# Table sets, first decays and the weight gathers of a one-core decoder layer: an order rewritten around the state scan

## The chip, the core and the metric

One core of a Trainium2 chip runs the whole layer as one program. The metric is device microseconds of one execution; lower is better. Engines are named as in the profile: PE (matrix multiply), DVE (vector), ACT (scalar functions), POOL (GpSimd), SP (a queue that only issues transfers). ACT and POOL issue transfers too.

## What is computed

The layer is `x = layernorm(x + f(x))` three times, on 4 x 256 tokens of width 256, for three functions `f`:

```
# 1: a state space block (512 channels, 16 states) and a mixture of experts behind it
x, z = split(rmsnorm(h) @ in_proj.T);  xc = silu(conv4(x) + conv_b)
dt, B, C = split(xc @ x_proj.T) ;  dt = softplus(rmsnorm(dt) @ dt_proj.T + dt_b)
h_t = h_{t-1} * exp(dt_t * A) + (dt_t * x_t) * B_t ;  y_t = sum_n h_t * C_t      # the scan
r = (y + xc * D) * silu(z) @ out_proj.T + h
logits = rmsnorm(r) @ router.T ; top 2 of 8 experts ; sum of w2(silu(w1 t) * w3 t)
# 2: cross attention over 64 keys, 16 heads
# 3: a feed forward block in fp8: columns of w_gate, w_up and w_down are reordered by index
#    tables, every row is scaled by its largest size and rounded to fp8
g = q(x[:, up]) @ q(w_gate[:, up]).T ; u likewise with w_up ; y = q((silu(g) * u)[:, down]) @ q(w_down[:, down]).T
```

Softplus is computed as `max(v, 0) + log(1 + exp(-|v|))`, so each part of `dt` passes through `Abs`, `Exp` and `Ln` on ACT, with a correction of the rounding on DVE between `Exp` and `Ln`.

## The kernel before

Each engine has its own program, written out by hand; semaphores order them against each other. The sequence has these stages.

**Projections (to 74 us).** The tokens are taken in two halves of 512, the 512 channels in four chunks of 128. ACT's order mixes `Silu` (convolution, `take_gates` 0 to 3), `Exp` (`dt_exponential`) and `Ln` (`dt_logarithm`). Whenever ACT needs a function that is not in the table set it holds, the compiler puts a table load ahead of it. On DVE `rounding_rest`, `softplus` and `scan_inputs` follow ACT; PE transposes the products `dt * x` (`transpose_inputs`) and `take_inputs` copies them from PSUM to SBUF as `dtxT`: tiles 0 to 3 on DVE, 4 to 7 on ACT.

**The scan (74 to 224 us).** There are 64 units: 2 halves x 16 states x 2 pairs of channel chunks. For each unit ACT makes the decays `exp(dt * A)` (`decay_of`, two instructions of 510 columns) and scales rows of `dtxT` by `B` (`input_rows`, three of 512 columns and one diagonal of 128 for each two units); PE turns these rows (`inputs_of`); DVE runs `tensor_tensor_scan` over 1024 columns (`scan_of`), with the decays from SBUF and the inputs from PSUM; POOL multiplies the states by `C` (line 470, 1024 columns, both operands in SBUF); PE adds the products up (`sum_states`). `decay_of(u)` waits for scan `u-2`, scan `u` for product `u-3`. The last product is done by DVE (`last_state_times_c`, line 1318).

**Behind the scan (224 to 258 us).** PE projects the gated result, DVE adds it to `x` and finds the two best experts of each token. From there DVE alone counts, ranks and places the tokens in a chain of small instructions, each waiting for the one before (lines 1341 to 1382; among them `place + behind`, line 1362, `picked * place`, line 1363, and 16 comparisons, line 1374). PE gathers from these marks the row indices, and POOL uses them in `gather_rows` (line 487), with which the experts begin.

**Weight gathers.** `w_up` and `w_gate` (6 chunks of 128 rows each) are gathered through `down_reorder_index` by POOL with one indirect transfer for each chunk. In this kernel POOL issues all 12 before the scan, into spare memory (`got`), because their final place `w_raw` is taken by `dt` until the last decay is made. Behind the scan `mask_up` multiplies them by a mask of columns into `w_raw` (lines 454), then `w_down` is masked (line 480), then come two small powers for the norm of the result (line 484). SP starts the load of the second expert's weights, which lie over part of `got`, when all three masks are done.

Of the kernel before, what the change touches and what calls it, by code (L numbers as in the profile page):

```python
# [43 lines left out]
KVT = BATCH * KV  # L44
FPAD = FCH * P
FP8_MAX = 448.0
SCALES = 2 * FCH + KD


# [17 lines left out]
def build(nc, inp, out):  # L67
    with ExitStack() as ctx:
# [116 lines left out]
        up_mask, down_mask = sb("up_mask", [P, D]), view(118, [FF], BF16)  # L185
        count_row = view(159, [FF + D], rows=1)
        w_raw = [view(72.5, [FCH, D]), view(78.5, [FCH, D]), view(112.5, [KD, FF])]
        got = [view(16.5, [FCH, D]), (view(146.5, [4, D]), view(22.5, [2, D]))]
        w_size = [view(66.5, [FCH * D]), view(66.5, [FCH * D]), view(66.5, [KD * FF])]
        w_fp8 = [view(34.5, [FCH, D], BF16), view(37.5, [FCH, D], BF16), view(181, [KD, FPAD], BF16)]  # L190
        w_fp8T = [view(73.5, [KD, FPAD], BF16), view(76.5, [KD, FPAD], BF16), view(84.5, [FCH, D], BF16)]
# [86 lines left out]
        def _(sp):  # L278
# [47 lines left out]
            for m in range(C_BUFS, 2 * NS):  # L326
                sp.wait_ge(s["hc_done"], 2 * (m - C_BUFS) + 2)
                load_c_row(m)
            sp.wait_ge(s["masked"], 3)
            load_weights(1)  # L330
            for half in range(2):
                tiles = slice(half * HALF_TILES, (half + 1) * HALF_TILES)
# [37 lines left out]
        def _(pool):  # L370
# [78 lines left out]
                    pool.indirect_dma_start(dst[:, c - chunks[0], :], None, inp[name], bass.IndirectOffsetOnAxis(gather_at[:, c:c + 1].bitcast(U32), 0))\  # L449
                        .then_inc(s[f"gathered_w{m}"], 16)  # L450

            def mask_up(dst, rows, chunks, gathered):
                pool.wait_ge(s[gathered], FCH * 16)
                pool.tensor_tensor(dst, rows, up_mask[:, :].unsqueeze(1).to_broadcast([P, chunks, D]), ALU.mult).then_inc(s["masked"], 1)

            pool.wait_ge(s["ld_idx"], 16)
            pool.wait_ge(s["xproj_psum"], 2 * CI)
            pool.wait_ge(s["dt_psum"], 2 * CI)
            gather_weights(1, "w_up", range(4), got[1][0])
            pool.wait_ge(s["z_psum"], TILES)  # L460
            gather_weights(1, "w_up", range(4, FCH), got[1][1])
            gather_weights(0, "w_gate", range(FCH), got[0])
            in_chunks = lambda v: v.rearrange("p (c t) -> p c t", c=2)
            for unit in range(UNITS - 1):
                m = unit // 2
# [6 lines left out]

            pool.wait_ge(s["da_ready"], UNITS)
            pool.wait_ge(s["scan_done"], UNITS + 1)
            mask_up(w_raw[1][:, 0:4, :], got[1][0], 4, "gathered_w1")
            mask_up(w_raw[1][:, 4:FCH, :], got[1][1], FCH - 4, "gathered_w1")
            mask_up(w_raw[0], got[0], FCH, "gathered_w0")
            pool.wait_ge(s["spread_done"], 2)
            pool.wait_ge(s["ld_late"], 32)
            pool.tensor_tensor(w_raw[2], w_raw[2], down_mask.unsqueeze(1).to_broadcast([P, KD, FF]), ALU.mult).then_inc(s["masked"], 1)  # L480
            for half in range(2):
                tiles = slice(half * HALF_TILES, (half + 1) * HALF_TILES)
                pool.wait_ge(s["ms_ready"], 7 + half)
                pool.tensor_tensor(rs[:, tiles], ms[:, tiles], neg_half[:, tiles], ALU.pow).then_inc(s["rstd"], 1)

            def gather_rows(index):
                pool.indirect_dma_start(row_in, None, hn_rows[:, :], bass.IndirectOffsetOnAxis(index, 0)).then_inc(s["ld_rows"], 16)  # L487
# [100 lines left out]
        def _(act):  # L588
# [67 lines left out]
            def dt_exponential(c, half):  # L656
                act.wait_ge(s["dt_act"], CI * half + c + 1)
                nc.scalar.activation(u[half][:, c, :], u[half][:, c, :], ACT.Exp, scale=-1.0).then_inc(s["dt_exp"], 1)
# [21 lines left out]
                for n in range(HALF_TILES, TILES):  # L680
                    nc.scalar.activation(zsT[:, n, :], zsT[:, n, :], ACT.Silu).then_inc(s["z_out"], 1)

            def take_inputs(i):
                act.wait_ge(s["dtxT_psum"], 2 * CI)
                tile = HALF_TILES + i
                nc.scalar.activation(dtxT[:, tile, :], ps[:, tile, :], ACT.Identity).then_inc(s["dtxT_done"], 1)


# [56 lines left out]
            take_dt(2, 0)  # L745
            convolved(2, 1)
            convolved(3, 1)
            dt_exponential(0, 0)
            squares_of_small(1)
            take_small(1)  # L750
# [6 lines left out]
            take_gates(1)  # L757
            take_gates(2)
            take_gates(3)
            dt_logarithm(0, 0)  # L760
            take_dt(0, 1)
            dt_logarithm(1, 0)
# [14 lines left out]
            dt_logarithm(0, 1)  # L777
            dt_logarithm(1, 1)
            take_gates(6)
            dt_logarithm(2, 1)  # L780
            dt_logarithm(3, 1)
            take_gates(7)
            act.wait_ge(s["routing"], RATES_READY)
            act.wait_ge(s["consts"], 5)
            act.wait_ge(s["softplus"], 2)
            decay_of(0)
            act.wait_ge(s["b_scaled"], 2)
            input_rows(0, range(HALF_TILES))
            act.wait_ge(s["softplus"], 4)
            decay_of(1)  # L790
            act.wait_ge(s["ld_idx"], 32)
            act.wait_ge(s["routing_psum"], 3)
            input_rows(1, range(HALF_TILES))
            for i in range(HALF_TILES):
                take_inputs(i)
            act.wait_ge(s["softplus"], 2 * CI)
            act.wait_ge(s["b_scaled"], 4)
            for unit in range(2, UNITS):
                decay_of(unit)
                if unit // 2 + 1 < 2 * NS:  # L800
                    input_rows(unit // 2 + 1, range(2 * (unit % 2), 2 * (unit % 2) + 2))

# [268 lines left out]
        def _(dve):  # L1071
# [126 lines left out]
                dve.wait_ge(s["conv_out"], n + 1)  # L1198
                nc.vector.tensor_tensor(dtx[half][:, c, :], dt[:, c, halves[half]], xc[:, c, halves[half]], ALU.mult).then_inc(s["dtx_done"], 1)

            def take_inputs(i):
                dve.wait_ge(s["dtxT_psum"], CI)
                nc.vector.tensor_copy(dtxT[:, i, :], ps[:, i, :]).then_inc(s["dtxT_done"], 1)

            def take_routing():
                dve.wait_ge(s["routing_psum"], 3)
                link(nc.vector.tensor_tensor(x_rms[:, :], ms[:, 0:TILES], rs[:, 0:TILES], ALU.mult))
# [47 lines left out]
            take_routing()  # L1255
            rounding_rest(2, 1)
            softplus(0, 1)
            take_inputs(0)
            take_inputs(1)
            take_inputs(2)  # L1260
            take_inputs(3)
            softplus(1, 1)
            scan_inputs(0, 1)
            scan_inputs(1, 1)
# [6 lines left out]
            def quantise(m, parts):  # L1271

                chunks, width = (FCH, FCH, KD)[m], (D, D, FF)[m]
                w, size = w_raw[m], w_size[m].rearrange("p (a b) -> p a b", b=width)
                largest, inverse, scale = (v[:, m, 0:chunks] for v in (w_max, w_inv, w_scale))
                if 1 in parts:
                    dve.wait_ge(s["masked"], (3, 2, 4)[m])
                    link(nc.vector.tensor_reduce(largest, w, axis=AX.X, op=ALU.max, apply_absolute_value=True))
                    link(nc.vector.tensor_scalar(scale, largest, 1.0 / FP8_MAX, None, ALU.mult))
                    link(nc.vector.reciprocal(inverse, scale))  # L1280
                if 2 in parts:
                    for c in range(chunks):
                        ins = nc.vector.tensor_scalar(w[:, c, :], w[:, c, :], inverse[:, c:c + 1], None, ALU.mult)
                    ins.then_inc(s["w_scaled"], 1)
                if 4 in parts:
                    dve.wait_ge(s["w_sized"], (2, 3, 1)[m])
                    link(nc.vector.scalar_tensor_tensor(w, size, LEAST_ADDED, w, ALU.max, ALU.add))
                if 5 in parts:
                    ins = nc.vector.scalar_tensor_tensor(w_fp8[m][:, :, 0:width], size, LEAST_ADDED, w, ALU.max, ALU.subtract)
# [1157 lines left out]
```

## Time and profile before

| | us |
|---|---|
| three runs: median (lowest to highest) | 630.99 (630.53 to 631.51) |
| the profiled execution, its own time | 630.9 |
| its span from first to last instruction | 628.9 |
| projections, up to the first scan | 74.3 |
| 64 scans and the last product, up to | 226.7 |
| first rows of the experts requested | 255.1 |

All times in the rows are microseconds from the start of the span. 2.0 us of the profiled execution lie outside the span. A timeline row gives the start, the time from the first instruction's start to the last one's end, engine, line, operation, output and inputs, the count, and in brackets the idle time before it and what ended that.

### The profile page before, as it was taken

The page shows a single profiled execution, that of the slowest core. Times are in us where ns is not written, and L with a number is a line of the kernel's source. Part 1 is how long each engine was busy: PE and PEld are TensorE (multiplying, and loading weights), DVE is VectorE, ACT ScalarE, POOL GpSimd, SP SyncE. Part 2 cuts the span into 40 slices and gives each one's busy share as a digit, 9 for nine tenths or more (in the row PEclk, how much of TensorE's full clock was granted, in tenths as well). Part 3 has the DMA queues.
Part 4 walks back from the last instruction along what each step waited for, and adds up shares of the span by engine and source line. Part 5 has one row for each costly group of instructions (what it writes and reads, how often), then busy time and mean ns, then how long its engine had stood idle before and what let it go on. Part 6 is the DMA issues. An engine that isn't in the chain of part 4 may idle for free.

```text
span 628.9 us, 10914 instructions
## 1 busy us (share of the span) xinstructions
PE 583.5 (93%) x3632; PEld 440.8 (70%) x3632; DVE 464.5 (74%) x786; ACT 385.7 (61%) x879; POOL 301.5 (48%) x242
## 2 busy tenths in 40 slices
PE   6999689998999999999999999999999999998774
PEld 3553589887998887597779779778845555665442
DVE  6989999999999976544553543553555789998875
ACT  5689899999999956522232231321745764687633
POOL 7022699999999991134232334344112332225201
PEclk9999899999999999999999999999999999999998
DMA  8001651111221108334441441441510000000001
GB/s 288 1 2 43 203 194 52 53 66 51 52 67 51 34 17 327 125 124 172 172 158 49 172 170 35 169 177 30 160 45 1 1 2 0 1 1 1 2 0 67
DMA packets 18432, 52.41 MB, mean 83 GB/s; under 512 B 3872, under 2 KB 9647, under 8 KB 16720
## 3 DMA queue, kind: packets, MB, share of 16 engines
q1 hardware_dynamic: 15344, 42.36, 19.3%
q0 software_dynamic: 2752, 7.34, 3.9%
q10 hardware_dynamic: 288, 2.10, 0.9%
q8 instruction: 26, 0.43, 0.3%
q14 instruction: 22, 0.18, 0.1%
HBM read 47.13 MB, written 4.67 MB: 82 GB/s over the span
## 4 chain that ended last, share of the span: by engine, by line
PE 69%; ACT 13%; DVE 10%; issue 5%; DMA 2%; POOL 1%; SPq 0%; POOLq 0%; DVEq 0%; ACTq 0%
PE ps L2165 12%; PE ps L2230 8%; ACT arena L699 7%; PE ps L2173 6%; PE ps L2219 4%; PE ps L2251 4%; ACT arena L714 3%; PE ps L1948 3%; PE ps L1933 3%; PE ps L2105 3%; PE ps L1982 2%; PE ps L1782 2%; PE ps L1791 2%; PE ps L2031 2%; PE ps L1935 2%
## 5 line engine op out<-in xcount | busy, mean ns | idle before, releaser
L470 POOL TENSOR_TENSOR arena<-arena 128x1024 f32<-128x1024 f32 x63 | 147.3, 2389 | 3.3 <-DVE arena L1301 3.0
L1301 DVE TENSOR_TENSOR_SCAN arena<-arena,ps 128x1024 f32<-128x1024 f32 x64 | 143.4, 2279 | 4.0 <-ACT arena L699 0.9
L699 ACT ACTIVATE arena<-arena,a_neg 128x510 f32<-128x510 f32 x128 | 84.5, 708 | 1.9 <-DVE arena L1301 1.7
L2165 PEld LDWEIGHTS ps<-arena 128*128 128x128 f32 x660 | 75.5, 192 | 3.5 <-issue 3.1
L2165 PE MATMUL ps<-arena 128*128 128x128 f32 x660 | 77.1, 276 | 0.0
L1933 PE MATMUL ps<-ident,arena 128*128 128x128 f32 x384 | 64.7, 278 | 9.9 <-ACT arena L710 8.5
L1948 PE MATMUL ps<-ident,arena 128*128 128x128 f32 x512 | 67.3, 273 | 2.5 <-DVE arena L1310 1.8
L910 ACT ACTIVATE arena<-ps 128x256 f32<-128x256 f32 x45 | 17.3, 384 | 82.1 <-PE ps L2165 82.1
L714 ACT ACTIVATE arena<-arena,b_tok 128x512 f32<-128x512 f32 x96 | 64.8, 708 | 0.0
L1948 PEld LDWEIGHTS ps<-ident,arena 128*128 128x128 f32 x512 | 57.8, 141 | 4.1 <-DVE arena L1310 1.3
L2230 PE MATMUL ps<-arena 128*128 128x512 f32 x128 | 58.2, 595 | 0.0
L1933 PEld LDWEIGHTS ps<-ident,arena 128*128 128x128 f32 x384 | 45.8, 143 | 14.6 <-ACT arena L710 12.8
L1935 PE MATMUL ps<-arena 128*128 128x128 f32 x256 | 50.0, 277 | 0.0
L549 POOL TENSOR_TENSOR q_rs<-q_ms,neg_half 128x16 f32<-128x16 f32 x8 | 23.6, 2948 | 50.8 <-DVE q_ms L1552 50.8
L936 ACT ACTIVATE arena<-ps 128x128 f32<-128x128 f32 x128 | 33.5, 279 | 22.1 <-PE ps L2230 22.1
L2173 PE MATMUL ps<-arena 128*128 128x256 f32 x180 | 41.3, 379 | 0.0
L2230 PEld LDWEIGHTS ps<-arena 128*128 128x128 f32 x128 | 23.5, 190 | 24.1 <-issue 21.3
L520 POOL DMA_INDIRECT moe_out<-arena,result_now x23 | 24.1, 1047 | 32.3 <-DVE arena L1488 20.5
L1935 PEld LDWEIGHTS ps<-arena 128*128 128x128 f32 x256 | 39.2, 193 | 0.0
L1480 DVE TENSOR_TENSOR arena<-arena,ps 128x256 f32<-128x256 f32 x30 | 12.6, 422 | 34.5 <-ACT arena L910 33.1
L2173 PEld LDWEIGHTS ps<-arena 128*128 128x128 f32 x180 | 33.0, 190 | 3.9
L487 POOL DMA_INDIRECT arena<-hn_rows,row_now x23 | 25.4, 1106 | 18.2 <-POOL row_now L505 18.2
(316 smaller groups left out, 1135.8 us busy)
## 6 DMA issues: line engine op xcount, KB each, us to landing
arena<-in_w_moe SPq DMA_DIRECT2D x8, 2176.0 KB, 9.0
arena<-c_dram SPq DMA_DIRECT2D x32, 256.0 KB, 3.2
arena<-in_w_o ACTq DMA_DIRECT2D x1, 2048.0 KB, 13.1
arena<-in_w_qT SPq DMA_DIRECT2D x1, 2048.0 KB, 10.0
arena<-in_w_q SPq DMA_DIRECT2D x1, 2048.0 KB, 8.0
arena<-moe_out SPq DMA_DIRECT2D x8, 256.0 KB, 4.5
x<-in_x SPq DMA_DIRECT2D x2, 512.0 KB, 4.6
arena<-in_w_in SPq DMA_DIRECT2D x2, 512.0 KB, 5.8
```

What stands on the lines that cost most here:

```text
L470: pool.tensor_tensor(in_chunks(hC[unit % 3]), in_chunks(h[unit % 3]), c_bc[:, m % C_BUFS, :].unsqueeze(1).to_broadcast([P, 2, HALF]), ALU. ...
L487: pool.indirect_dma_start(row_in, None, hn_rows[:, :], bass.IndirectOffsetOnAxis(index, 0)).then_inc(s["ld_rows"], 16)
L699: ins = nc.scalar.activation(dA_b[:, unit % 2, 2 * k:2 * k + 2, 1:], dt_b[:, c, 2 * half:2 * half + 2, 1:], ACT.Exp, scale=a_neg[:, c, n:n ...
L714: nc.scalar.activation(sdtx[m % 2][:, i, :], dtxT[:, HALF_TILES * half + i, :], ACT.Identity, scale=b_tok[:, HALF_TILES * half + i, n:n + ...
L936: ins = nc.scalar.activation(q_junk[:, g % 2, hd * DH:(hd + 1) * DH], ps[:, g % 2, hd * DH:(hd + 1) * DH], ACT.Square, scale=float(DH) ** ...
L1301: nc.vector.tensor_tensor_scan(h[unit % 3], dA[:, k, :], ps[:, 2 * k:2 * k + 2, :].rearrange("p a b -> p (a b)"), 0.0, ALU.mult, ALU.add). ...
L1933: ins = nc.tensor.transpose(dst, sdtx[m % 2][:, i, c * P:(c + 1) * P], ident[:, :])
L1935: ins = nc.tensor.matmul(dst, dtxT[:, HALF_TILES * half + i, c * P:(c + 1) * P], b_diag[m % 2], start=True, stop=True)
L1948: return nc.tensor.matmul(ps[:, bank, c * P:(c + 1) * P], part, ident[:, :], start=first, stop=last, is_transpose=ADD_TRANSPOSED, skip_gro ...
L2165: ins = nc.tensor.matmul(ps[:, bank, c * P:(c + 1) * P], w13[:, k, chunk * P:(chunk + 1) * P], xT[:, k, :], start=(k == 0), stop=(k == KD ...
L2173: ins = nc.tensor.matmul(ps[:, 6, 0:D], hid[:, c, :], w2[:, c, :], start=(c == 0), stop=(c == FCH - 1))
L2230: ins = nc.tensor.matmul(ps[:, g % 2, :], tokens(t, k), w_q[:, k, g * HALF:(g + 1) * HALF], start=(k == 0), stop=(k == KD - 1))
```

## The change

- ACT is told twice to load a set that holds both `Exp` and `Ln`: ahead of the first `dt_exponential` and, behind the `Silu` of the gates, ahead of the first `dt_logarithm`.
- On ACT `decay_of(0)` and `decay_of(1)` come ahead of the last two logarithms; the copies `take_inputs` of tiles 0 to 3 leave DVE and come on ACT ahead of the first `input_rows`; those of tiles 4 to 7 come behind `decay_of(2)`.
- Before the scan POOL gathers only four chunks of `w_up`. The other two and all six of `w_gate` are gathered behind the scan, straight into `w_raw`, where they are masked in place. POOL's order behind the scan becomes: mask four chunks, gather 2 + 4, power of the first half, gather 2, mask two chunks, power of the second half, mask `w_down`, mask the six chunks of `w_gate`.
- SP starts the load of the second expert when 63 products are done.

```
@@ POOL, before the scan
-            gather_weights(1, "w_up", range(4), got[1][0])
-            pool.wait_ge(s["z_psum"], TILES)
-            gather_weights(1, "w_up", range(4, FCH), got[1][1])
-            gather_weights(0, "w_gate", range(FCH), got[0])
+            gather_weights(1, "w_up", range(4), got_up)
@@ POOL, behind the scan
             pool.wait_ge(s["scan_done"], UNITS + 1)
-            mask_up(w_raw[1][:, 0:4, :], got[1][0], 4, "gathered_w1")
-            mask_up(w_raw[1][:, 4:FCH, :], got[1][1], FCH - 4, "gathered_w1")
-            mask_up(w_raw[0], got[0], FCH, "gathered_w0")
+            mask_up(w_raw[1][:, 0:4, :], got_up, "gathered_w1", 4)
+            gather_weights(1, "w_up", range(4, FCH), w_raw[1][:, 4:FCH, :])
+            gather_weights(0, "w_gate", range(4), w_raw[0][:, 0:4, :])
+            rstd_of_result(0)
+            gather_weights(0, "w_gate", range(4, FCH), w_raw[0][:, 4:FCH, :])
+            mask_up(w_raw[1][:, 4:FCH, :], w_raw[1][:, 4:FCH, :], "gathered_w1", FCH)
+            rstd_of_result(1)
             pool.wait_ge(s["spread_done"], 2)
             pool.wait_ge(s["ld_late"], 32)
             pool.tensor_tensor(w_raw[2], w_raw[2], down_mask..., ALU.mult).then_inc(s["masked"], 1)
-            for half in range(2):
-                ...
+            mask_up(w_raw[0], w_raw[0], "gathered_w0", FCH)
@@ SP
-            sp.wait_ge(s["masked"], 3)
+            sp.wait_ge(s["hc_done"], UNITS - 1)
             load_weights(1)
@@ ACT
+            nc.scalar.preload_act_table_set(EXP_AND_LOG)
             dt_exponential(0, 0)
...
+            nc.scalar.preload_act_table_set(EXP_AND_LOG)
             dt_logarithm(0, 0)
...
             take_gates(6)
-            dt_logarithm(2, 1)
-            dt_logarithm(3, 1)
-            take_gates(7)
...
             decay_of(0)
+            act.wait_ge(s["softplus"], 4)
+            decay_of(1)
+            dt_logarithm(2, 1)
+            dt_logarithm(3, 1)
+            take_gates(7)
+            for i in range(HALF_TILES):
+                take_inputs(i)
             act.wait_ge(s["b_scaled"], 2)
             input_rows(0, range(HALF_TILES))
-            act.wait_ge(s["softplus"], 4)
-            decay_of(1)
...
             input_rows(1, range(HALF_TILES))
-            for i in range(HALF_TILES):
-                take_inputs(i)
...
                 decay_of(unit)
+                if unit == 2:
+                    for i in range(HALF_TILES, TILES):
+                        take_inputs(i)
@@ DVE: the four take_inputs between softplus(0, 1) and softplus(1, 1) are gone;
   quantise waits for "masked" 4, 2, 3 (w_gate, w_up, w_down) in place of 3, 2, 4
```

## Rows read from the trace of the kernel before

**Rows 1.** The page's chain that ended last, by engine.
```profile
PE 69%; ACT 13%; DVE 10%; issue 5%; DMA 2%; POOL 1%; SPq 0%; POOLq 0%; DVEq 0%; ACTq 0%
```

**Rows 2.** The chain of waits from 222 to 262 us: start, length, what.
```profile
223.64 1.97 DVE arena L1318
...
251.81 2.35 PE ps L2051 x16
...
255.10 3.09 DMA arena<-hn_rows,row_of
```

**Rows 3.** ACT's timeline ahead of the scan and in its first units.
```profile
55.45 1.28 ACT L658 ACT_TABLE_LOAD   x1
...
61.38 1.28 ACT L662 ACT_TABLE_LOAD   x1
...
66.07 1.28 ACT L699 ACT_TABLE_LOAD   x1
...
70.44 0.39 ACT L710 ACTIVATE arena<-ident,b_tok 128x128 f32<-128x128 f32 x1
...
76.27 2.06 ACT L686 ACTIVATE arena<-ps 128x512 f32<-128x512 f32 x4 [2.09 <-PE ps L1841]
...
80.65 1.33 ACT L699 ACTIVATE arena<-arena,a_neg 128x510 f32<-128x510 f32 x2
```

**Rows 4.** DVE's timeline up to the first scans.
```profile
66.68 2.47 DVE L1203 COPY arena<-ps 128x512 f32<-128x512 f32 x4
...
73.63 0.23 DVE L1167 TENSOR_TENSOR b_tok<-b_tok,rs 128x64 f32<-128x64 f32 x1
74.29 4.46 DVE L1301 TENSOR_TENSOR_SCAN arena<-arena,ps 128x1024 f32<-128x1024 f32 x2 [0.44 <-PE ps L1935]
79.65 33.06 DVE L1301 TENSOR_TENSOR_SCAN arena<-arena,ps 128x1024 f32<-128x1024 f32 x14 [0.89 <-ACT arena L699]
```

**Rows 5.** PE's timeline around the first scans.
```profile
70.41 1.72 PE L1841 MATMUL ps<-ident,arena 128*128 128x128 f32 x8 [4.28 <-DVE arena L1199]
...
82.94 0.55 PE L1933 MATMUL ps<-ident,arena 128*128 128x128 f32 x3 [1.87 <-ACT arena L710]
```

**Rows 6.** Windows of PE: length, busy, granted clock, DMA share, GB/s.
```profile
71.00:72.00 1.00, 1.00 (x7) 0.50 0.09 20
```

**Rows 7.** POOL's timeline: last gather, products of the scan, masks, powers.
```profile
73.99 0.94 POOL L449 DMA_INDIRECT arena<-in_w_gate,index_at  x1 [0.30 <-issue]
...
82.02 77.61 POOL L470 TENSOR_TENSOR arena<-arena 128x1024 f32<-128x1024 f32 x33 [0.65 <-DVE arena L1301]
...
226.81 6.99 POOL L454 TENSOR_TENSOR arena<-arena,up_mask 128x1024 f32<-128x1024 f32 x3 [1.22 <-issue]
233.76 2.86 POOL L480 TENSOR_TENSOR arena<-arena 128x1408 f32<-128x1408 f32 x1
239.63 1.04 POOL L484 TENSOR_TENSOR rs<-ms,neg_half 128x4 f32<-128x4 f32 x1 [3.01 <-DVE ms L1330]
246.37 1.01 POOL L484 TENSOR_TENSOR rs<-ms,neg_half 128x4 f32<-128x4 f32 x1 [5.70 <-DVE ms L1330]
```

**Rows 8.** DVE's timeline behind the scan: the last product and two placing steps.
```profile
223.64 3.04 DVE L1318 TENSOR_TENSOR arena<-arena 128x1024 f32<-128x1024 f32 x1
...
247.92 0.23 DVE L1362 TENSOR_TENSOR place<-place,behind 128x64 f32<-128x64 f32 x1
248.18 0.29 DVE L1363 TENSOR_TENSOR picked<-picked,place 128x128 f32<-128x128 f32 x1
```

**Rows 9.** Line 1561: duration in ns, least, median and most, of eight.
```profile
L1561 DVE TENSOR_TENSOR arena<-arena,total_e x8: 1224/1226/2066, 478.0 to 587.1; 128x1024 f32<-128x1024 f32 x8
```

**Rows 10.** DVE's timeline, 536 to 542 us, attention and feed forward.
```profile
539.17 2.07 DVE L1561 TENSOR_TENSOR arena<-arena,total_e 128x1024 f32<-128x1024 f32 x1
```

**Rows 11.** POOL's timeline, 476 to 560 us, the same place.
```profile
538.48 1.67 POOL L560 TENSOR_TENSOR arena<-arena 128x704 f32<-128x704 f32 x1 [6.95 <-ACT arena L963]
```

**Rows 12.** Line 449, the weight gathers: time from issue to landing.
```profile
DMA to landing us min/median/max: 2.7/3.0/10.2
```

More of the change, by code:

```diff
@@ L46 @@
 FP8_MAX = 448.0
+EXP_AND_LOG = "natural_log_exp_and_others"
 SCALES = 2 * FCH + KD
@@ L187, in build @@
         w_raw = [view(72.5, [FCH, D]), view(78.5, [FCH, D]), view(112.5, [KD, FF])]
-        got = [view(16.5, [FCH, D]), (view(146.5, [4, D]), view(22.5, [2, D]))]
+        got_up = view(146.5, [4, D])
         w_size = [view(66.5, [FCH * D]), view(66.5, [FCH * D]), view(66.5, [KD * FF])]
@@ L450, in gather_weights, with mask_up @@
                         .then_inc(s[f"gathered_w{m}"], 16)
-            def mask_up(dst, rows, chunks, gathered):
-                pool.wait_ge(s[gathered], FCH * 16)
-                pool.tensor_tensor(dst, rows, up_mask[:, :].unsqueeze(1).to_broadcast([P, chunks, D]), ALU.mult).then_inc(s["masked"], 1)
+            def mask_up(dst, rows, gathered, landed):
+                pool.wait_ge(s[gathered], landed * 16)
+                pool.tensor_tensor(dst, rows, up_mask[:, :].unsqueeze(1).to_broadcast([P, rows.shape[1], D]), ALU.mult).then_inc(s["masked"], 1)
             pool.wait_ge(s["ld_idx"], 16)
@@ L474, in _, with rstd_of_result @@
             pool.wait_ge(s["scan_done"], UNITS + 1)
-            mask_up(w_raw[1][:, 0:4, :], got[1][0], 4, "gathered_w1")
-            mask_up(w_raw[1][:, 4:FCH, :], got[1][1], FCH - 4, "gathered_w1")
-            mask_up(w_raw[0], got[0], FCH, "gathered_w0")
+            mask_up(w_raw[1][:, 0:4, :], got_up, "gathered_w1", 4)
+            gather_weights(1, "w_up", range(4, FCH), w_raw[1][:, 4:FCH, :])
+            gather_weights(0, "w_gate", range(4), w_raw[0][:, 0:4, :])
+            def rstd_of_result(half):
+                tiles = slice(half * HALF_TILES, (half + 1) * HALF_TILES)
+                pool.wait_ge(s["ms_ready"], 7 + half)
+                pool.tensor_tensor(rs[:, tiles], ms[:, tiles], neg_half[:, tiles], ALU.pow).then_inc(s["rstd"], 1)
+            rstd_of_result(0)
+            gather_weights(0, "w_gate", range(4, FCH), w_raw[0][:, 4:FCH, :])
+            mask_up(w_raw[1][:, 4:FCH, :], w_raw[1][:, 4:FCH, :], "gathered_w1", FCH)
+            rstd_of_result(1)
             pool.wait_ge(s["spread_done"], 2)
@@ L480, in _ @@
             pool.tensor_tensor(w_raw[2], w_raw[2], down_mask.unsqueeze(1).to_broadcast([P, KD, FF]), ALU.mult).then_inc(s["masked"], 1)
-            for half in range(2):
-                tiles = slice(half * HALF_TILES, (half + 1) * HALF_TILES)
-                pool.wait_ge(s["ms_ready"], 7 + half)
-                pool.tensor_tensor(rs[:, tiles], ms[:, tiles], neg_half[:, tiles], ALU.pow).then_inc(s["rstd"], 1)
+            mask_up(w_raw[0], w_raw[0], "gathered_w0", FCH)
             def gather_rows(index):
@@ L681, in late_gates, with take_inputs @@
                     nc.scalar.activation(zsT[:, n, :], zsT[:, n, :], ACT.Silu).then_inc(s["z_out"], 1)
-            def take_inputs(i):
-                act.wait_ge(s["dtxT_psum"], 2 * CI)
-                tile = HALF_TILES + i
+            def take_inputs(tile):
+                act.wait_ge(s["dtxT_psum"], CI if tile < HALF_TILES else 2 * CI)
                 nc.scalar.activation(dtxT[:, tile, :], ps[:, tile, :], ACT.Identity).then_inc(s["dtxT_done"], 1)
@@ L1199, in scan_inputs @@
                 nc.vector.tensor_tensor(dtx[half][:, c, :], dt[:, c, halves[half]], xc[:, c, halves[half]], ALU.mult).then_inc(s["dtx_done"], 1)
-            def take_inputs(i):
-                dve.wait_ge(s["dtxT_psum"], CI)
-                nc.vector.tensor_copy(dtxT[:, i, :], ps[:, i, :]).then_inc(s["dtxT_done"], 1)
             def take_routing():
@@ L1257, in _ @@
             softplus(0, 1)
[L1258 to L1261, printed above, removed]
             softplus(1, 1)
@@ L1276, in quantise @@
                 if 1 in parts:
-                    dve.wait_ge(s["masked"], (3, 2, 4)[m])
+                    dve.wait_ge(s["masked"], (4, 2, 3)[m])
                     link(nc.vector.tensor_reduce(largest, w, axis=AX.X, op=ALU.max, apply_absolute_value=True))
```

## The prediction

> **What bounds the kernel now.** I read the page's chain first: PE carries most of it [rows 1], so any delay ahead of the experts goes through PE to the end. The change touches two stretches, so next came the timelines of ACT, DVE and PE up to the first scans, and of POOL and DVE behind the scan, with the chain of waits there.
>
> In the first stretch ACT works without a break and pays 1.28 us for each table load, three of them after 55 us [rows 3]. DVE has its own work done at 73.86 [rows 4]. The first scan, at 74.29, waits 0.44 us for PE [rows 4]; PE had stood still for 4.28 us and then ran at a granted clock of 0.50, which is 1.2 of 2.4 GHz [rows 5, 6]. The third scan waits another 0.89 us for its decays [rows 4], because ACT's copies of tiles 4 to 7, from 76.27, are ahead of them [rows 3].
>
> In the scan itself POOL has no room: 33 products in 77.61 us are 2.35 each [rows 7], against 2.36 for DVE's early scans (33.06 for 14) [rows 4]. What comes earlier at its start comes earlier at its end.
>
> Behind it the chain runs over the last product, PE's projections, and then DVE's placing steps, PE's 16 small matmuls at 251.81 and the request for rows at 255.10 [rows 2]. POOL has done its masks by 236.62 (233.76 + 2.86) and then waits for DVE [rows 7]: its masks end long before DVE's first placing step.
>
> **The change, part 1: the start of the scan.** *ACT.* From the first of the three loads, 55.45, to the end of the first diagonal, 70.73, ACT needs 15.28 us [rows 3]. Three loads with their gaps of 0.02 go: -3.9. Two things are moved ahead: one more pair of decays, about 1.22 by the pitch of such pairs (1.33 from first start to last end, less 0.1 of overlap), and four copies, 2.06 [rows 3]. 55.45 + 15.28 - 3.9 + 1.22 + 2.06 = 70.1. Being earlier, ACT meets PE's results at two places (the rows of C and the seventh gate); I add 0.3: 70.4. The two early decays wait for nothing late, since the first half of `dt` is done by then; behind them the two logarithms meet DVE's second rounding steps, which finish at about the same time.
>
> *DVE.* Four copies go. They take 2.47 us, 2.4 of pitch [rows 4], so DVE is ready at 73.86 - 2.4 = 71.5. *PE.* The transposes that waited for DVE come 2.4 us earlier, and PE's break ahead of them shrinks from 4.28 to about 1.9. After a break of 1.87 us three transposes took 0.55 us, full speed [rows 5]. The inputs of the first unit then start at 70.4, with ACT's diagonal, and take some 1.15 us, to 71.6: the first scan starts at 71.7, 2.6 us earlier. If PE is at half clock still, add 1.15: 72.8.
>
> *The next scans.* Its first scan ends at 71.7 + 2.23 (half of 4.46 [rows 4]) = 73.95. Then ACT makes decays (1.22), four copies (2.06), two rows (1.22), decays (1.22): 79.7 for the decays of the fourth unit. Before, that pair began at 80.65 [rows 3] and was done at 81.87. The order behind it is as before, so the gain that stays is **2.15 us**; the wait of 0.89 has only moved from the third scan to the fourth. Bounds: 1.1 with PE at half clock, 2.4 if nothing but DVE's copies counted. POOL agrees: its fourth product starts at about 82.15 instead of 82.02 + 2.35 = 84.37. POOL's eight gathers ahead of the scan end at 74.93 [rows 7]; they had to go, as the first product is wanted at 73.95, a cost of 1.0 avoided, not a further gain.
>
> The Trainium skill, "ScalarE: Activation LUTs", section "What ACT_TABLE_LOAD costs", gives 2.66 us for a switch with a drain of 1.38. This trace shows 1.28 and the next instruction 0.02 behind it. By the page ACT would come 4.1 us earlier still, and the scan would start with DVE at 71.5 in place of 71.7.
>
> **Part 2: POOL behind the scan** (times of the kernel before; all of it moves 2.15 earlier together). The masks take 6.99 us for 3072 columns, 2.28 ns each [rows 7]. From 226.81: mask of four chunks 2.33, to 229.1. Six gathers, 0.94 plus 0.30 of issue [rows 7], 7.5 with their first, to 236.7. The first power waits until 239.63 as before: cover 2.9 us. Two gathers, to 243.2; mask of two chunks 1.17, to 244.4. The second power starts at 246.37 as before: cover 2.0, so the norm and the stored rows are not late. Up to here the moved work costs nothing; without the covers it would be paid in full.
>
> Then come the mask of `w_down`, 247.4 to 250.3, and that of six chunks of `w_gate`, 1536 x 2.28 = 3.5 us, to 253.8. Both read two operands from SBUF, and now run beside DVE's placing steps, which begin at 247. Three rows show what that does. Line 1318, two SBUF operands of 1024 columns, took 3.04 us while POOL's last product ran [rows 8]; line 1561, the same shape, takes 1.23, except 2.07 in the worst case [rows 9], and that one started at 539.17 inside a POOL product from 538.48 to 540.15 [rows 10, 11]: 540.15 + 1.23 is its end within 0.15. So DVE waited for the end of POOL's instruction each time.
>
> Line 1362 (two SBUF operands, 247.92 [rows 8]) would therefore wait from 247.9 to 250.3, and line 1363, 0.26 behind it, for the second mask: 250.5 + 3.5 = 254.0 instead of 248.18 [rows 8]. The chain behind it is unhindered again. Term: **+5.8 us**. It hardly matters who wins between the masks, since the chain can't be through before the second has ended. Bounds: 5.4 if `w_gate` runs at the rate of `w_down` (2.86 for 1408 columns, 2.03 ns: 3.1 us [rows 7]), 6.0 if DVE is caught a step earlier; 0 if small steps are let through, which no row shows. I take 5.8, as every row of this pair of engines is a full wait. Queued behind: PE waits with its 16 matmuls [rows 2], POOL's own request for rows waits for DVE anyway, and ACT's exponential for the router waits with them.
>
> The Trainium skill, "SBUF — State Buffer", section "Who interferes with whom", has this as a rule: a DVE instruction with two SBUF inputs and a GpSimd instruction that reads SBUF exclude each other for the whole instruction. It speaks against this change; by it the sum is the one I make, without it 5.8 less.
>
> PE's break ahead of line 2051 grows from nothing to 5 us. After 4.28 us it ran at half clock [rows 5, 6]; the 16 matmuls take 2.35 us [rows 2] beside comparisons that DVE makes at about that pace. I take +0.4, between 0 and 2.3 (all of them twice as long).
>
> **At nothing:** the earlier load of the second expert (only earlier, and what SP has queued behind it waits for the norm anyway); the mask of `w_down` as third, since it is first wanted inside the experts; the load of `w_o`, which waits for the first mask, still the first.
>
> **Sum.** The profiled execution took 630.9 us, 628.9 of them its span; the median is 630.99, so nothing is to be corrected. 630.9 - 2.15 + 5.8 + 0.4 = **634.9 us**. Its own range: 630.9 - 2.4 + 5.4 = 633.9 to 630.9 - 1.1 + 6.0 + 2.3 = 638.1.
>
> **Rivals.** *A, the other side: DVE passes POOL.* If small placing steps aren't held up by the masks, only part 1 is left: 630.9 - 2.15 = 628.75. For it: the rows of waits are of 1024 columns, these steps have 64 and 128. Against it: a wait for a port doesn't ask how long the waiting one is. It decides once the hold is under 2.15 us.
>
> *B, only one mask bites.* Gathers land in 2.7 to 10.2 us [rows 12]; the last two are issued by 243.2, beside the load of `w_o`. If they land at about 253, DVE is held for the first mask alone, 2.4 us, and goes through before the second: 630.9 - 2.15 + 2.4 = 631.15. Against it: the median is 3.0 [rows 12].
>
> *C, the scan does not start earlier*, because the compiler puts loads back or ACT's new order is late elsewhere, while the masks bite: 630.9 + 5.8 + 0.4 = 637.1. Against it: PE's and DVE's waits at 74 go by count.
>
> **Chances.** About 0.2%, 1.3 us, is what a measurement of this kernel tells from no change. The forecast has 0.69, A 0.16, B 0.11, C 0.04. Faster 0.16 (A); same 0.11 (B); slower 0.73 (forecast and C). The range runs from 631.0 to 637.2: it takes in B, the forecast and C, and leaves out A and the top of the bounds.
>
> **What would show it.** Right: no table load on ACT between 50 and 74; the first scan near 71.7, a wait of about 1.3 ahead of the fourth; the last product some 2 us earlier; then line 1362 at about 2.6 us, line 1363 at about 3.5, PE standing still 5 us ahead of line 2051, and the first request for rows 3 to 4 us later than 255.10. Wrong: lines 1362 and 1363 at their old 0.23 and 0.29, or the second mask behind the request for rows.

## The result and the profile after

The changed kernel is slower: 639.09 us (median of four runs, 637.55 to 640.18) against 631.25 (median of four, 630.53 to 635.53). The ratio is 1.0105, 95% interval 1.007 to 1.0139. Forecast were 634.9 and a range up to 637.2: the sign came as forecast, and so did the hold of VectorE behind the scan, but the gain in the scan did not stay, and the time lies above the range.

The profiled execution took 639.09 us, its span 637.1. In the rows of after most line numbers are one higher than in those of before, POOL's and ACT's by other small amounts.

ACT's timeline ahead of the scan, answering to [rows 3]:

```profile
49.58 1.28 ACT L765 ACT_TABLE_LOAD   x1
50.88 0.63 ACT L667 ACTIVATE arena<-arena 128x512 f32<-128x512 f32 x1
...
70.41 0.41 ACT L714 ACTIVATE arena<-ident,b_tok 128x128 f32<-128x128 f32 x1
...
79.01 1.33 ACT L703 ACTIVATE arena<-arena,a_neg 128x510 f32<-128x510 f32 x2
```

The load at 49.58 is the last one, and the three behind 55 us are gone. The first diagonal is done at 70.82 (forecast 70.4), the fourth unit's decays at 80.34 (forecast 79.7); 0.48 us of each was lost ahead of the first `Exp` table load.

DVE's timeline, answering to [rows 4, 8]:

```profile
72.24 6.64 DVE L1302 TENSOR_TENSOR_SCAN arena<-arena,ps 128x1024 f32<-128x1024 f32 x3 [0.43 <-PE ps L1936]
80.43 4.52 DVE L1302 TENSOR_TENSOR_SCAN arena<-arena,ps 128x1024 f32<-128x1024 f32 x2 [1.55 <-ACT arena L703]
86.30 68.70 DVE L1302 TENSOR_TENSOR_SCAN arena<-arena,ps 128x1024 f32<-128x1024 f32 x30 [1.35 <-PE ps L1936]
...
157.29 2.28 DVE L1302 TENSOR_TENSOR_SCAN arena<-arena,ps 128x1024 f32<-128x1024 f32 x1
160.82 63.85 DVE L1302 TENSOR_TENSOR_SCAN arena<-arena,ps 128x1024 f32<-128x1024 f32 x28 [1.25 <-PE ps L1936]
224.70 2.69 DVE L1319 TENSOR_TENSOR arena<-arena 128x1024 f32<-128x1024 f32 x1
...
248.64 2.43 DVE L1363 TENSOR_TENSOR place<-place,behind 128x64 f32<-128x64 f32 x1
251.10 3.41 DVE L1364 TENSOR_TENSOR picked<-picked,place 128x128 f32<-128x128 f32 x1
...
260.95 0.19 DVE L1383 SCALAR_TENSOR_TENSOR result_of<-ps,row_of 128x34 uint32<-128x34 f32 x1
```

Read the brackets from above. The first scan starts 2.05 us earlier than in [rows 4]. The fourth, at 80.43, waits 1.55 for its decays. Then come two waits that before does not have, both for PE: 1.35 ahead of the sixth scan and 1.25 in the middle. So the last product, which began at 223.64 [rows 8], begins at 224.70, later and not earlier. Below it the two placing steps are held 2.43 and 3.41 us, where they took 0.23 and 0.29.

POOL's timeline behind the scan, answering to [rows 7]; POOL's mask at 248.13 and the next at 250.95 end where the two DVE steps end:

```profile
240.35 1.04 POOL L480 TENSOR_TENSOR rs<-ms,neg_half 128x4 f32<-128x4 f32 x1 [3.09 <-DVE ms L1331]
...
247.09 1.05 POOL L480 TENSOR_TENSOR rs<-ms,neg_half 128x4 f32<-128x4 f32 x1 [1.93 <-DVE ms L1331]
248.13 2.85 POOL L488 TENSOR_TENSOR arena<-arena 128x1408 f32<-128x1408 f32 x1
250.95 3.41 POOL L455 TENSOR_TENSOR arena<-arena,up_mask 128x1536 f32<-128x1536 f32 x1
261.20 1.05 POOL L492 DMA_INDIRECT arena<-hn_rows,row_of  x1 [6.84 <-DVE result_of L1383]
```

Ahead of both powers POOL still waits for DVE, 3.09 and 1.93 us: the covers of the forecast, 2.9 and 2.0.

PE's timeline at the scan's start and behind the placing steps, answering to [rows 5]:

```profile
70.88 0.55 PE L1934 MATMUL ps<-ident,arena 128*128 128x128 f32 x3 [1.17 <-ACT arena L714]
...
81.30 0.55 PE L1934 MATMUL ps<-ident,arena 128*128 128x128 f32 x3 [2.29 <-ACT arena L714]
...
82.46 1.87 PE L1949 MATMUL ps<-ident,arena 128*128 128x128 f32 x8
...
86.10 1.04 PE L1949 MATMUL ps<-ident,arena 128*128 128x128 f32 x8
...
257.56 2.67 PE L2052 MATMUL ps<-arena 128*128 128x68 bf16 x16 [5.03 <-DVE arena L1375]
...
260.39 5.14 PE L2032 MATMUL ps<-arena 128*64 128x256 f32 x32
```

Windows of PE in the same places (start:end, length, busy, granted clock, DMA share, GB/s):

```profile
82.00:84.00 2.00, 2.00 (x14) 0.62 0.25 91
84.00:86.00 2.00, 2.00 (x12) 0.52 0.00 1
158.00:160.00 2.00, 2.00 (x12) 0.50 0.29 97
160.00:162.00 2.00, 2.00 (x16) 0.75 0.03 8
```

For comparison before's window in the middle, then its rows of PE there and for the 32 matmuls of the values, and last after's rows of PE in the middle:

```profile
158.00:160.00 2.00, 1.98 (x18) 1.00 0.53 128
```

```profile
156.31 0.30 PE L1948 MATMUL ps<-ident,arena 128*128 128x128 f32 x1 [1.08 <-DVE arena L1310]
...
158.02 0.77 PE L1948 MATMUL ps<-ident,arena 128*128 128x128 f32 x5 [0.27 <-DVE arena L1310]
...
254.28 3.67 PE L2031 MATMUL ps<-arena 128*64 128x256 f32 x32
```

```profile
155.73 0.30 PE L1949 MATMUL ps<-ident,arena 128*128 128x128 f32 x1 [1.08 <-DVE arena L1311]
...
157.43 1.22 PE L1949 MATMUL ps<-ident,arena 128*128 128x128 f32 x5 [0.27 <-DVE arena L1311]
```

After a break of 2.29 us ahead of 81.30 the clock falls to half in the first microseconds of work, and the same eight transposes that take 1.04 us at 86.10 take 1.87 at 82.46. The window 158 to 160 shows a second fall, where before has 1.00. Ahead of this one PE's breaks are the same in both kernels: 1.08, 0.20, 0.27 and 0.27 us. Behind the placing steps PE stands still for 5.03 us; the 16 small matmuls then take 2.67 us and the 32 of the values 5.14, where before had 3.67.

For what follows the span is cut into six stretches: **A** to the first `Exp` table load, **B** to the first scan, **C** to the last product, **D** to the places of the rows (`result_of`), **E** to the first store of an expert's rows, **F** to the end. Each is the difference of two starts in the profile of one execution. The labels are those of the experiments.

| us | A | B | C | D | E | F | span |
|---|---|---|---|---|---|---|---|
| before | 38.99 | 35.30 | 149.35 | 31.21 | 15.76 | 358.29 | 628.9 |
| before_again | 39.23 | 35.55 | 149.63 | 31.18 | 15.76 | 360.35 | 631.7 |
| before_third | 38.67 | 35.55 | 154.26 | 30.89 | 15.75 | 359.98 | 635.1 |
| after | 39.47 | 32.77 | 152.46 | 36.25 | 17.22 | 358.93 | 637.1 |
| after_again | 39.00 | 32.77 | 152.29 | 36.29 | 17.08 | 358.87 | 636.3 |
| act_only | 40.57 | 32.77 | 152.27 | 30.86 | 15.79 | 359.74 | 632.0 |
| pool_only | 38.68 | 35.25 | 149.35 | 36.57 | 16.81 | 359.24 | 635.9 |
| masks_late | 38.55 | 33.85 | 152.65 | 30.85 | 17.57 | 360.23 | 633.7 |
| one_mask | 38.95 | 33.39 | 150.66 | 34.02 | 16.83 | 359.85 | 633.7 |
| no_stand | 40.60 | 33.55 | 149.78 | 36.49 | 17.44 | 360.74 | 638.6 |
| keep_busy | 41.98 | 32.76 | 150.22 | 36.27 | 18.39 | 359.28 | 638.9 |
| act_busy | 39.08 | 32.76 | 150.23 | 30.87 | 15.82 | 360.64 | 629.4 |
| act_busy_again | 39.03 | 33.84 | 150.40 | 30.89 | 15.92 | 361.02 | 631.1 |
| mended | 39.38 | 32.76 | 150.23 | 30.88 | 15.94 | 360.81 | 630.0 |

From before to after the 8.2 us of span are A +0.48, B -2.53, C +3.11, D +5.04, E +1.46, F +0.64. A and F contain nothing that the change touches: over the three executions of before A spans 0.56 us and F 2.06. Over all fourteen A runs from 38.55 to 41.98, though every kernel has the same work there.

### The profile page after: what moved, and what is told of

Same layout as the page of the kernel before. It is cut to its first block, busy times and chain, and to the rows that moved or that the text cites. A ratio compares the mean times of both kernels' runs of the same rounds, so it can differ in the third digit from the quotient of the medians.

```text
span 637.1 us, 10911 instructions
## 1 busy us (share of the span) xinstructions
PE 587.7 (92%) x3632; PEld 444.6 (70%) x3632; DVE 468.1 (73%) x782; ACT 384.0 (60%) x880; POOL 299.0 (47%) x242
## 4 chain that ended last, share of the span: by engine, by line
PE 67%; ACT 14%; DVE 10%; issue 5%; DMA 2%; POOL 0%; SPq 0%; POOLq 0%; DVEq 0%; ACTq 0%
PE ps L2166 11%; PE ps L2231 9%; ACT arena L703 7%; PE ps L2174 6%; PE ps L2220 4%; ACT arena L718 4%; PE ps L1949 3%; PE ps L2252 3%; PE ps L1934 3%; PE ps L1983 2%; PE ps L1783 2%; PE ps L2032 2%; PE ps L2106 2%; PE ps L1792 2%; PE ps L1936 2%
## 5 line engine op out<-in xcount | busy, mean ns | idle before, releaser
L1934 PE MATMUL ps<-ident,arena 128*128 128x128 f32 x384 | 65.4, 280 | 11.1 <-ACT arena L714 9.8
L1949 PE MATMUL ps<-ident,arena 128*128 128x128 f32 x512 | 68.7, 277 | 2.3 <-DVE arena L1311 1.8
L1949 PEld LDWEIGHTS ps<-ident,arena 128*128 128x128 f32 x512 | 59.2, 143 | 3.8 <-DVE arena L1311 1.3
L1934 PEld LDWEIGHTS ps<-ident,arena 128*128 128x128 f32 x384 | 46.3, 144 | 15.8 <-ACT arena L714 14.0
```

What stands on the lines that cost most here:

```text
L1934: ins = nc.tensor.transpose(dst, sdtx[m % 2][:, i, c * P:(c + 1) * P], ident[:, :])
L1949: return nc.tensor.matmul(ps[:, bank, c * P:(c + 1) * P], part, ident[:, :], start=first, stop=last, is_transpose=ADD_TRANSPOSED, skip_gro ...
```

## The experiments

The times and ratios are against the kernel before, run beside each experiment; the stretches are those of one profiled execution.

**The two parts apart.** `act_only` is before with ACT's and DVE's part of the change; `pool_only` is before with POOL's and SP's.

> The kernel before with the table sets, the order on ACT and the copies alone; POOL gathers before the scan as it did. Theory H/C (the gain at the scan's start is lost again in the scan, to the later fourth scan and to PE at half clock): first scan about 2.5 us earlier than before, end of scan no earlier than before, nothing behind the scan changes; 630 to 632. Rival G (the gain was lost because of the moved gathers and the earlier load of the second expert): here the scan keeps its 2 us, 629 or less; against it, POOL's gathers end 1 us after the first product is wanted.

> The kernel before with POOL's and SP's part alone. Theory H: the scan as before, the placing chain held by 5.5 us and PE's half clock 1.4 behind it: about 631 + 6.9 = 638. If the loss behind the scan needed ACT's part too: 631 to 633.

`act_only`: 631.80 us against 631.51, ratio 0.9994 (0.9974 to 1.0014). `pool_only`: 638.77, ratio 1.0122 (1.0087 to 1.0157). The loss comes with POOL's part alone, and the gain of ACT's part does not reach the end. In the table B of `act_only` is 2.5 us shorter, as in after, and C 2.9 us longer; `pool_only` has B and C of before, D of after, and 1.05 us of the 1.46 that E gains in after. DVE's timeline of `pool_only`, the two placing steps:

```profile
247.53 2.42 DVE L1366 TENSOR_TENSOR place<-place,behind 128x64 f32<-128x64 f32 x1
249.99 3.42 DVE L1367 TENSOR_TENSOR picked<-picked,place 128x128 f32<-128x128 f32 x1
```

**Both masks later.** `masks_late` is after with the masks of `w_down` and `w_gate` behind the second request for rows:

```
             rstd_of_result(1)
-            pool.wait_ge(s["spread_done"], 2)
-            pool.wait_ge(s["ld_late"], 32)
-            pool.tensor_tensor(w_raw[2], w_raw[2], down_mask..., ALU.mult).then_inc(s["masked"], 1)
-            mask_up(w_raw[0], w_raw[0], "gathered_w0", FCH)
...
             gather_rows(row_of[:, 1:2])
+            ... (the same four lines)
```

> The changed kernel with one thing moved: the masks of w_down and of the six chunks of w_gate come behind the second request for rows. Theory H (the two masks hold DVE's placing steps, and PE's stand-still then costs half clock): the steps place+behind and picked*place are back at 0.2 to 0.3 us, the first request for rows comes about 5.5 us earlier, PE's values-times-output stretch is back from 5.07 to 3.7 us; time about 639 - 5.5 - 1.4 = 632. Rival T (the transfers now behind the scan, gathers and the second expert's weights, delay what the placing needs): no change, 637 to 640.

634.55 us, ratio 1.0047 (1.003 to 1.0065). The placing steps are back at 0.23 and 0.29 us, D at 30.85 and the 32 matmuls of the values at 3.67, so the moved transfers are not what delayed the placing. But E is 17.57, 1.8 more than before, and the time misses the expected 632. DVE's row and POOL's rows there:

```profile
260.57 6.74 DVE L1457 TENSOR_TENSOR prob<-prob,stat 128x64 f32<-128x64 f32 x1
```

```profile
260.96 2.86 POOL L497 TENSOR_TENSOR arena<-arena 128x1408 f32<-128x1408 f32 x1
263.77 3.44 POOL L455 TENSOR_TENSOR arena<-arena,up_mask 128x1536 f32<-128x1536 f32 x1
267.16 0.19 POOL L510 COPY row_now<-row_of 128x1 uint32<-128x1 uint32 x1
```

The hold has only moved: a step of DVE with two SBUF operands, the router's division, now lasts 6.74 us, to the end of the second mask at 267.2. It starts 0.39 us ahead of the first mask and takes 0.22 in `act_busy`, and was held all the same; no run shows why. The step behind it had 4.11 us to spare in `act_busy`, so only a part of this is paid.

**One mask earlier.** `one_mask` is after with the mask of `w_down` ahead of the first power, in the break of 3.09 us, and only that of `w_gate` left in its place (`quantise` waits for 4, 3, 2).

> The changed kernel with the mask of w_down moved ahead of the first power, into POOL's break of 3 us there; the mask of w_gate stays behind the second power. Theory H (each mask holds DVE for as long as it runs): place+behind is held for about 3 us by the one mask that is left, picked*place is back at 0.3; the placing chain is 2.4 us shorter than in the changed kernel; 635 to 637, the lower end if PE's shorter stand-still costs no half clock. Rival (a fixed price for running beside POOL, whatever is left of it): the sum of the two steps stays near 5.8 us.

636.40 us, ratio 1.0069 (1.0045 to 1.0093). DVE's placing steps:

```profile
247.24 3.02 DVE L1363 TENSOR_TENSOR place<-place,behind 128x64 f32<-128x64 f32 x1
250.29 0.29 DVE L1364 TENSOR_TENSOR picked<-picked,place 128x128 f32<-128x128 f32 x1
```

One mask holds one step, for its own rest: POOL's mask ran from 246.73 to 250.17. D is 34.02, 2.8 over before, and E 1.07 over it: dose and effect for the hold, and for PE's half clock behind it, which came after a break of 2.50 us.

**PE kept at work in the scan.** `keep_busy` is after with 16 transposes of the identity ahead of the inputs of unit 4 (the fifth), and 4 behind each of the gates in the middle. They fill PE's breaks and their results are overwritten. `act_busy` is the same on top of `act_only`.

```
+                if unit == 4:
+                    pe.wait_ge(s["scan_done"], unit - 1)
+                    for _ in range(16):
+                        nc.tensor.transpose(ps[:, 0, 0:P], ident[:, :], ident[:, :])
...
+                    for _ in range(4):
+                        nc.tensor.transpose(ps[:, HALF_TILES + i, 0:P], ident[:, :], ident[:, :])
```

> The changed kernel with added transposes on PE whose results are overwritten: 16 ahead of the inputs of the fifth unit, and 4 behind each of the four gates between the halves. They stand where PE otherwise waits. Theory C (PE's half clock at 82.6 to 86 and at 158 to 161 us costs the scan about 1.3 and 1.2 us): the clock stays at 1.00 through the scan, the waits of 1.35 and 1.25 ahead of two scans go, the last product comes 2 to 2.5 us earlier, time about 636.5; the half clock behind the placing stays. Rival (the scan's loss is ACT's and POOL's own): the added work changes nothing or costs up to 1 us, 639 to 640.

> The part of ACT and DVE alone, POOL as before the change, with PE kept busy at the two places as in the earlier experiment. Theory C (half clock on PE ate the 2 us of the scan's start): first scan to last product within 151 us instead of 152.5, nothing changed behind; about 2 us less than the kernel before, 629.5. Rival (ACT's order loses it by itself): no less than the kernel before.

C is 150.22 and 150.23 where it was 152.46 and 152.27: with the clock held up 2.2 and 2.0 us are gone, and 0.9 us over before is left. DVE's timeline of `act_busy`, and from before the scans in front of the middle, in one row:

```profile
80.04 73.53 DVE L1298 TENSOR_TENSOR_SCAN arena<-arena,ps 128x1024 f32<-128x1024 f32 x32 [1.56 <-ACT arena L699]
...
158.35 63.69 DVE L1298 TENSOR_TENSOR_SCAN arena<-arena,ps 128x1024 f32<-128x1024 f32 x28 [0.20 <-PE ps L1936]
```

```profile
79.65 75.93 DVE L1301 TENSOR_TENSOR_SCAN arena<-arena,ps 128x1024 f32<-128x1024 f32 x33 [0.89 <-ACT arena L699]
```

Of the long waits only that for the fourth unit's decays, 1.56, is left, against 0.89 in [rows 4]: from the first scan to the fourth are 8.20 us, 0.48 over before. The other half of the 0.9 stands with the added transposes: from the end of the 35th scan (153.57; in before 79.65 + 75.93 = 155.58) to the last product are 68.50 us, where before has 68.06 and `no_stand`, without transposes there, 68.05. Both places were filled at once, so it is not tested whether the second fall comes without the first. The whole times did not follow: `keep_busy` 640.40 where about 636.5 was expected (ratio 1.0144, 1.0104 to 1.0184), its profile with A 2.5 and E 1.2 us over those of after; `act_busy` 632.52 against 632.03, where 629.5 was expected (1.0006, 0.9983 to 1.0029).

**The stand-still behind the placing steps.** `no_stand` is after with 40 transposes of the identity ahead of the 16 small matmuls, so that PE works through the hold.

> The changed kernel with 40 added transposes on PE, into a bank that is free then, where PE otherwise stands still for 5 us ahead of the 16 small matmuls. Theory K (the stand-still brings half clock, and that alone makes the stretch behind it 1.4 us longer): clock 1.00 from 253 us on, values-times-output back at 3.7 us, the hold of DVE unchanged; about 1.4 us less than the changed kernel. Rival: that stretch is long because the rows come late; no change.

642.27 us, ratio 1.0161 (1.0099 to 1.0222), where 1.4 us less than after were expected. The theory fell here. PE's timeline and windows:

```profile
251.87 4.53 PE L2052 MATMUL ps<-ident 128*128 128x128 f32 x40
257.09 2.64 PE L2055 MATMUL ps<-arena 128*128 128x68 bf16 x16 [0.69 <-DVE arena L1375]
...
259.86 5.36 PE L2032 MATMUL ps<-arena 128*64 128x256 f32 x32
```

```profile
259.00:260.00 1.00, 1.00 (x15) 1.00 0.00 0
260.00:261.00 1.00, 1.00 (x8) 0.55 0.00 0
261.00:262.00 1.00, 1.00 (x8) 0.50 0.00 0
```

The break is down to 0.69 us and the clock holds at 1.00 to 260, but it falls then all the same, in the middle of unbroken work, and E is 17.44. Filling the stand-still was not enough to hold the clock; what sets the fall there is not shown.

**Everything mended.** `mended` is after with the transposes of `keep_busy`, the mask of `w_down` early as in `one_mask`, and that of `w_gate` behind the second request as in `masks_late`.

> The whole change, with PE kept busy at the two places in the scan, the mask of w_down in POOL's break ahead of the first power and the mask of w_gate behind the second request for rows. Theory H with C: no step of the placing held, scan 2 us earlier, and with one mask only between the requests for rows the third request is not late: 629.5, below both kernels. Rival (masks there delay the experts by 3 us, as both together did): 631.5 or more.

633.69 us, ratio 1.0036 (1.001 to 1.0062). 629.5 had been expected. B to E are as in `act_busy`, 1.8 us less than in the first profile of before, but F is 360.81; the mask of `w_gate` still holds the router's division, for 3.94 us, inside the time it has to spare. No version tried beats the kernel before beyond the measurement.

**The same kernels again.** The stretches of unchanged kernels, one execution each.

> The kernel before, unchanged, to see how far its own stages vary. In its first profile the stretch from the first Exp table load to the first scan took 35.30 us, first scan to last product 149.35, last product to the expert rows' places 31.21, and from there to the end 374.05; in every changed kernel that last stretch was 375.5 to 378.2. If the last stretch varies by itself with what the experts' transfers meet, this run shows more than 374.05, up to 376 or so, and nothing of the change explains it. If the change lengthens it, this run shows 374.05 within 0.5. The scan's stretch should be 149.35 within 0.3 in either case, as the part with POOL's move alone had the same.

> The kernel before a third time, for the same question: with the two others it gives the spread of each stretch. Varying by itself: the three values of the last stretch lie over 1 us apart. Lengthened by the change: all three lie at 374.05 within 0.5.

> The changed kernel, unchanged, a second time. The hold of VectorE's two placing steps is fixed by the order of the queues: it should be there again, 2.4 and 3.4 us within 0.2. Where TensorE falls to half clock depends on how long it was idle and is not fixed: by the theory that the scan's loss is that half clock, the stretch from first scan to last product is anything from 149.8 (no wait at the scan's start and in its middle) to 152.7, and its excess over 149.35 is the 0.7 to 0.9 of the late fourth scan plus the waits for TensorE that the row of the scans names. The rival, that the scan is slower for a reason of its own, has 152.46 again with other waits.

> ScalarE's part alone, with the extra transposes that keep TensorE at work, a second time. Scan start 32.76 us behind the first Exp table load, first scan to last product 150.23, both within 0.3, if the extra transposes hold the clock up each time. The last stretch was 376.46: by the theory that it varies by itself it lies anywhere from 374 to 378; by the rival it stays at 376.5 within 0.5.

633.54 and 637.15 us for before, 638.06 for after, 633.00 for `act_busy`. F of before was 358.29, 360.35 and 359.98: it varies by itself, and the first profile, the base of the sum, has the lowest F of all fourteen. The hold of after came again, 2.43 and 3.42 us, and so did C, 152.29, with waits of 0.39, 0.89 and 1.25 for PE. C of before, expected at 149.35 within 0.3, was 149.63 in the one and 154.26 in the other; B of `act_busy_again`, expected at 32.76 within 0.3, was 33.84. In the third execution of before the scan shows what both of after show. DVE's timeline and PE's row:

```profile
80.60 4.71 DVE L1301 TENSOR_TENSOR_SCAN arena<-arena,ps 128x1024 f32<-128x1024 f32 x2 [1.91 <-ACT arena L699]
86.32 2.29 DVE L1301 TENSOR_TENSOR_SCAN arena<-arena,ps 128x1024 f32<-128x1024 f32 x1 [1.01 <-PE ps L1935]
90.08 68.69 DVE L1301 TENSOR_TENSOR_SCAN arena<-arena,ps 128x1024 f32<-128x1024 f32 x30 [1.47 <-PE ps L1935]
...
164.45 64.00 DVE L1301 TENSOR_TENSOR_SCAN arena<-arena,ps 128x1024 f32<-128x1024 f32 x28 [1.11 <-PE ps L1935]
```

```profile
83.89 0.90 PE L1933 MATMUL ps<-ident,arena 128*128 128x128 f32 x3 [2.88 <-ACT arena L710]
```

PE's break at this place, ahead of the diagonal of the third pair of units, sorts the executions without extra transposes: 1.86, 1.87 and 2.15 us (`pool_only` and two of before) with no fall of the clock; 2.29 in five (after twice, `act_only`, `one_mask`, `no_stand`), 2.40 in `masks_late` and 2.88 in the third of before, of which all but `no_stand` fell.

The fall in the middle is not sorted so. It came in after twice, `act_only`, `masks_late` and the third of before, and not in the first two of before, `pool_only`, `one_mask` and `no_stand`; the breaks ahead of it are the 1.08, 0.2, 0.27 and 0.27 us of above in all ten. `one_mask` has the first fall without the second.

There is a third place. In four of the ten executions with ACT's part (`masks_late`, `one_mask`, `no_stand`, `act_busy_again`) PE was at half clock for the inputs of the first units; their first scan waited 1.06 to 1.51 us for PE, and B is 0.6 to 1.1 us longer. DVE's row of `act_busy_again`:

```profile
72.87 4.46 DVE L1298 TENSOR_TENSOR_SCAN arena<-arena,ps 128x1024 f32<-128x1024 f32 x2 [1.30 <-PE ps L1936]
```

PE's breaks ahead of it, 1.92 and 1.09 us, are those of `act_busy`, 1.92 and 1.08, which did not fall.

## Why the prediction was wrong in size

*Start of the scan, -2.15: the start came, the gain did not stay.* With A's 0.48 taken off, ACT's 70.4 was 70.34 and the first scan's 71.7 was 71.76, 2.53 us shorter from the first `Exp` load. That PE was at full clock there was partly luck: four of ten executions had the half clock that the forecast kept as a bound (72.8). The fourth scan waited 1.55 (forecast about 1.3) and came, with A's 0.48 taken off, 2.06 us earlier than in [rows 4] (79.65 + 33.06 / 14 = 82.01, against 80.43). Up to there the sum holds.

The step that failed is "The order behind it is as before, so the gain that stays is 2.15 us". The order did stay; PE's clock did not. The forecast used the three fast transposes behind 1.87 us [rows 5] for the break ahead of the first inputs, and priced no break and no half clock further on in the scan. The half clock then cost 1.35 us at the sixth scan, of which the scans behind it made up 0.35 (the 32 from the fourth on took 74.57 us, in before 73.57), and 1.25 in the middle with 0.4 more behind it. B and C together are +0.58 and not -2.15. That it is the half clock, `keep_busy` and `act_busy` show, and `no_stand`, in which neither of the two came, has C at 149.78: with B of after that would be -2.10, the forecast's gain. What set the clock down is only in part traced: ahead of the first fall the fourth unit's lateness had grown PE's break from 1.87 to 2.29 us, ahead of the second no break had grown.

*The wait behind the scan, +5.8: right in kind, a little high.* Both masks held DVE, each one step, in the order forecast. The two lines alone are 2.43 + 3.41 - 0.23 - 0.29 = +5.32, just under the lower bound of 5.4: the forecast let line 1363 begin when the second mask ended, and it was done 0.15 us behind that end. D as a whole is +5.04: the 16 matmuls add 0.16, and the last product, now 2.69 us for 3.04, takes off 0.35. Rivals A and B fall with it: DVE does not pass POOL, even with 64 columns, and both masks bite. `one_mask` measured B's case: 2.8 us in D and 1.1 in E, where 2.4 was the price. Rival C's condition did not come either: no load came back, and the first scan was early.

The Trainium skill, "SBUF — State Buffer", section "Who interferes with whom", has the exclusion as a rule for a whole instruction without regard to size. The traces agree down to 64 columns: 2.43, 3.02, 3.94 and 6.74 us for steps of about 0.23. They don't for a step of 8 columns with two SBUF operands that runs inside POOL's power (128 x 4, also two SBUF operands), and before has that too, in 246.37 to 247.38 [rows 7]:

```profile
247.12 0.17 DVE L1356 TENSOR_TENSOR_SCAN count<-ones,count 128x8 f32<-128x8 f32 x1
```

So "every row of this pair of engines is a full wait" holds for the rows that the forecast read.

*PE behind the placing steps, +0.4: under-sized.* The 16 matmuls were priced; they took 2.67 us for 2.35 to 2.51. Not priced were the 32 of the values behind them, which ran in part at half clock too: 5.14 for 3.67. E is +1.46. In after twice, `pool_only`, `one_mask` and `no_stand` what E has over before is what these 32 matmuls have over 3.67, within 0.03: 1.46, 1.32, 1.05, 1.07 and 1.68 us.

*At nothing:* the covers of both powers were 3.09 and 1.93 us, and nothing in front of the masks was late. `act_only` and `pool_only` add up to the change: +0.29 and +7.26, against 7.84.

With the measured stretches the sum is 630.9 + 0.58 + 5.04 + 1.46 + 0.48 + 0.64 = 639.1 us, as it must be, since they add up to the span. The miss of 4.2 is 2.73 in the scan, 1.46 in E, 1.12 in A and F, less 1.16 in D (5.04 for 5.8 + 0.4).

*Open:* what makes the clock fall in the middle of the scan, at its start in some executions, and in the middle of work in `no_stand`; and where the gain of `act_busy` goes. Its two profiles have B to E together 0.6 to 2.4 us below the first two of before, but F at 360.64 and 361.02, 0.3 us or more over all three of before. Whether F is longer for a reason, two profiles do not tell.

## What to carry to other kernels

A vector step with two SBUF operands, here of 64 and 128 columns, can cost as much as the GpSimd instruction that it meets, so list what runs beside each GpSimd instruction that is moved, and look for the next such step too when one is cleared. A gain at the start of a pipeline can be lost further on: follow the moved wait to TensorE's break, and price every matmul behind that break at both clock levels, not only the first ones. Profile the unchanged kernel more than once before a sum is made on one execution of it: here two untouched stretches of the kernel before varied by 0.6 and 2.1 us, and its scan by 4.9.

## What was not expected of the hardware

- The same break of 2.29 us at the same place was followed by half clock in four executions of five; the same small breaks in the middle of the scan (1.08, 0.2, 0.27, 0.27) by half clock in some executions and not in others.
- Filling a stand-still of 5.03 us down to 0.69 did not hold TensorE's clock: it fell 3 us later, from 1.00 to 0.50, without any break in between.
- POOL's small power (128 x 4, 1.05 us) ran just ahead of these masks without a visible hold of DVE: the step that was held 2.43 us began at 248.64, 0.51 behind the start of the mask, and those before it took their usual 0.17 to 0.23.
- The kernel before, unchanged, gave 629.9 to 637.2 us, and its slowest profiled execution lost 4.6 to 4.9 us against the two others in the scan alone, in the same waits for PE as the changed kernel.
